# Second graph layer: the order of TensorE's edge products and of ScalarE's message scaling within a turn

## The reference, cut to what matters

```
h  = relu(layernorm(x))
h  = relu([h, mean of h[src] over dst, mean of h[dst] over src] @ W1 + b1)
y  = x + [h, mean of h[src] over dst, mean of h[dst] over src] @ W2 + b2
h2 = relu(layernorm(y))
agg = segment_sum(edge_attr, dst)
out = y + mlp([h2, agg, u])          # 256, 256, 128; leaky relu
```

## Time and profile before

| what | us |
|---|---|
| median of 3 runs | 4304.13 |
| lowest and highest run | 4294.77, 4335.73 |
| the profiled execution, its own time | 4353.21 |
| span of that execution | 4351.6 |
| granted TensorE clock, mean share of full speed | 0.93 |

### The profile page before, as it was taken

How to read it: one execution, slowest core, us unless ns; L and a number is a source line. 1 busy time by engine, 2 the same in 40 slices (tenths; PEclk the granted TensorE clock), 3 DMA queues, 4 the chain that set the end, 5 groups by cost and what they waited for, 6 DMA issues and landing times.

```text
span 4351.6 us, 100093 instructions
## 1 busy us (share of the span) xinstructions
PE 3767.9 (87%) x25698; PEld 3324.9 (76%) x25698; DVE 3179.5 (73%) x11005; ACT 2323.0 (53%) x5788; POOL 3002.4 (69%) x2962
## 2 busy tenths in 40 slices
PE   3385899899999688888888888879999999999999
PEld 0123788888888678887788788768888888888888
DVE  3284788888888555555555555569999999999998
ACT  0001444444444455555555555557777777777776
POOL 6614787787777677777777777756666666666665
PEclk6687999999999899999999999989999999999999
DMA  7714777777777577777777777767777777777765
GB/s 278 272 58 161 176 171 175 180 173 179 171 175 177 132 179 179 186 184 187 177 181 183 178 182 186 173 144 159 158 160 157 159 159 158 160 158 158 159 158 124
DMA packets 818323, 742.05 MB, mean 171 GB/s; under 512 B 200444, under 2 KB 629896, under 8 KB 818282
## 3 DMA queue, kind: packets, MB, share of 16 engines
q1 hardware_dynamic: 637702, 522.72, 40.8%
q0 software_dynamic: 166208, 167.10, 26.3%
q10 hardware_dynamic: 14372, 51.75, 3.0%
HBM read 355.07 MB, written 334.83 MB: 159 GB/s over the span
## 4 chain that ended last, share of the span: by engine, by line
PE 47%; issue 5%; another core or an unknown queue 4%; ACT 3%; DVE 3%; DMA 2%; SPq 1%; POOL 0%; ACTq 0%; DVEq 0%; POOLq 0%
PE bank L1559 8%; PE bank L1573 4%; PE bank L1572 4%; PE bank L1574 4%; PE bank L1444 3%; PE bank L1467 3%; PE bank L1468 3%; PE bank L1478 2%; PE bank L1537 2%; PE bank L1530 2%; PE bank L1536 2%; PE bank L1532 2%; PE bank L1531 2%; PE bank L1546 2%
## 5 line engine op out<-in xcount | busy, mean ns | idle before, releaser
L626 POOL DMA_INDIRECT node<-summed,rep_index x392 | 628.0, 1602 | 266.3 <-issue 129.4
L579 POOL DMA_INDIRECT sums<-summed,rep_index x392 | 620.7, 1583 | 166.9 <-issue 127.7
L657 POOL TENSOR_TENSOR resid<-node_out,b3s 128x128 f32<-128x128 f32 x784 | 336.7, 460 | 478.3 <-DVE rows L1281 474.9
L1231 DVE SCALAR_TENSOR_TENSOR z<-bank,bias,small 128x512 f32<-128x512 f32 x784 | 567.9, 744 | 67.6 <-ACT small L889 58.7
L889 ACT ACTIVATE small<-bank,bias_small 128x512 f32<-128x512 f32 x784 | 535.2, 683 | 106.8 <-PE bank L1574 59.3
L1467 PE MATMUL bank<-hx,W1s 128*128 128x128 f32 x1568 | 345.1, 306 | 221.5 <-ACT hx L830 179.8
L667 POOL TENSOR_TENSOR z_lo<-z,z_hi 128x512 fp32r<-128x512 f32 x392 | 496.4, 1287 | 9.5 <-ACT z_hi L920 9.5
L611 POOL DMA_INDIRECT ends<-sums,index x392 | 382.0, 974 | 121.9 <-issue 120.1
L1467 PEld LDWEIGHTS bank<-hx,W1s 128*128 128x128 f32 x1568 | 268.6, 215 | 254.5 <-issue 254.1
L1559 PE MATMUL bank<-w3s,z 128*128 128x128 f32 x3136 | 382.4, 275 | 3.1 <-DVE z L1231 3.1
L1559 PEld LDWEIGHTS bank<-w3s,z 128*128 128x128 f32 x3136 | 365.7, 192 | 4.1 <-DVE z L1231 4.0
(11 more groups left out here) (152 smaller groups left out, 9727.2 us busy)
## 6 DMA issues: line engine op xcount, KB each, us to landing
node<-blank SPq DMA_DIRECT2D x98, 768.0 KB
sums<-zeros ACTq DMA_DIRECT2D x98, 512.0 KB
normed<-in_x_dram SPq DMA_DIRECT2D x196, 256.0 KB
rows<-sums SPq DMA_DIRECT2D x196, 256.0 KB
y<-node_out SPq DMA_DIRECT2D x196, 256.0 KB
node_out<-node SPq DMA_DIRECT2D x196, 256.0 KB, 3.2
node_out<-y POOLq DMA_DIRECT2D x196, 256.0 KB, 4.2
a_parts<-a_pair SPq DMA_DIRECT2D x784, 64.0 KB, 2.5
```

The lines of the kernel that those rows point to most:

```text
L579: pool.indirect_dma_start(sums1, bass.IndirectOffsetOnAxis(ap=rep_index[:, b, s:s + 1], axis=0), summed[:, b, s, 0:F], None, compute_op=AL ...
L626: pool.indirect_dma_start(node1, bass.IndirectOffsetOnAxis(ap=rep_index[:, b, s:s + 1], axis=0), summed[:, b, s, :], None, compute_op=ALU. ...
L1231: dve.scalar_tensor_tensor(out=z[:, m, :], in0=bank[first_bank + m][:], scalar=bias[:, m:m + 1], in1=small[:, m, :], op0=ALU.add, op1=ALU. ...
```

## The change

Two moves, one in each of two streams; no instruction is added or removed.

- TensorE: `end_products`(g+1) goes from just behind `sums`(g) to just behind `x_transposes`(g+1, 1). The preactivations of block 0 and the transposes of block 1 so come ahead of it.
- ScalarE: `end_messages`(g+1) goes from just behind `normalised`(g+1, 1) to just behind `hidden_x`(g+1, 1), the last place but one of the turn.

```diff
@@ scalar stream, layer2, step @@
                         hidden_x(g + 1, 1 - b, 0)
                         end_rows(g + 1, 1 - b)
                         normalised(g + 1, 1 - b, 1)
-                        end_messages(g + 1, 1 - b)
                     if second:
                         root(g + 2, b, 0)
                     if follows:
                         hidden(g + 1, 1 - b, 0)
                         hidden_x(g + 1, 1 - b, 1)
+                        end_messages(g + 1, 1 - b)
                     if second:
                         normalised(g + 2, b, 0)
@@ tensor stream, layer2, step @@
                     sums(g, b, uses)
                     if follows:
-                        end_products(*ahead)
                         preactivations(*ahead, uses + b, 0)
                         x_transposes(*ahead, 1)
+                        end_products(*ahead)
                     node_products(g, b, 1)
```

## The result

The changed kernel takes 4295.12 us (median of 10 runs, 4276.09 to 4303.86), the kernel before 4319.72 (10 runs, 4294.77 to 4335.73). The ratio is 0.9935, with a 95% interval of 0.9915 to 0.9955: 0.65% faster, 28 us by the ratio and 25 by the medians. The forecast was 4299 us, 5 us under a median of three runs that lay low; seven more runs moved the median of before up by 16 us. The time was met, and the difference was five times the one forecast.

The account below looks back on a forecast made before the run. The prediction took a 12.30 us ring around block 0's x load, plus late events, to hold the 14.10 us turn. Its terms summed to -11 us, half expected lost: -5 us on 4304.13, hence 4299, 8-in-10 range 4245 to 4350.

Parts of the forecast that it names:

- ScalarE, the gain: ScalarE, messages taken from ahead of block 0's root: about 0.9 us gained in one turn of eight, 11 us in all.
- The forecast's own sign: In the changed kernel's trace: block 0's root directly behind `normalised`, with a wait longer by about 1.1 us.
- the guess of one turn in eight: Share of turns where block 0's root has its input ready when the messages end; bounds none and one in three.
- TensorE, priced at nothing: TensorE, block 0's preactivations and block 1's transposes start 0.91 us earlier but meet ScalarE at the root: no gain.
- rival A: Faster: `hidden`'s 47 unexplained waits shrink by 0.91 us each, 43 us (4261), at most 112.4 us (4192); chance 0.22.
- The covers: Slack before TensorE's transposes takes up ScalarE's later work: 1.32 us, 0.29 left; if gone, up to 101 us slower.
- Rival B: Slower: ScalarE's messages wait in their new place for late edge products, past 0.29 us of cover: 51 us (4355); chance 0.15.
- The ring around the x load: Chain from `node_rows` through block 0's x load, statistics and root back to `node_rows`: 12.30 us of the 14.10 us turn.
- Rival C: Faster: the messages' 1.12 us leave the path to `hx` in each turn, 110 us (4194); chance 0.02.

Follow-up runs that it names:

- The filler: The changed kernel with four activations that nobody reads put at the messages' old place, ahead of the root of block 0: 4282.29 us, ratio 0.9909.

## Why the prediction was right, and where it was not

The time lay in the range, and the size of the effect under the 1% that the forecast called no change. That 4299 came within 4 us of 4295.12 is luck: the base was 16 us too low and the gain 20 us too small, and the two errors nearly cancelled. The turn of 13.72 us stayed just inside the 13.7 at which the forecast would have failed. Point by point:

- **ScalarE, the gain.** "The root could start 1.1 us earlier if its input were there. It is not." The filler confirms it: 1.2 us of work put back there is free. The forecast's own sign held too: the root of block 0 waited 102 us in the stage before and 262 after, 1.7 us a turn more. Even the guess of one turn in eight was met, by 12 of 96. What the term left out is the wait ahead of the messages. The step priced `end_messages` by its 1.12 us and not by what it waits for: with a late completion the messages and the root come one after the other behind it, where now the root is done before. That wait was in the trace of before (37.9 us in the stage), and I had passed over it. ScalarE's half measured 11 to 20 us, where the sum had 11 and halved it.
- **TensorE, priced at nothing.** "The earlier `c_pre` and `c_xT` meet a ScalarE that stands at the root: nothing." This is the step that failed. With ScalarE's half in place, the earlier completions took `hidden`'s unexplained waits from 78 us to 39.4 and 26.3, and the time down by about 0.4%, 17 us. It is the mechanism of rival A, of which the prediction had worked out 43 us for its near end; TensorE's half gave two fifths of that, and only with ScalarE's half beside it. Alone it cost 43 to 48 us, which no part of the prediction foresaw. The waits also did not shrink each by 0.91 us, as A had it: there were 18 where there had been 47, at the same 2.2 to 2.4 us each, and part of them came up at the messages. The row of the changed kernel that answers to the earlier trace rows:

```profile
L838 ACT ACTIVATE hT<-bank,b1col x196: 667/687/707, 1465.4 to 2791.4; 128x512 f32<-128x512 f32 x196
...
  remote: 39.4, 18
```

- **The covers.** The 0.29 us left before the transposes held only in part. TensorE's transposes waited for `resid` 24.0 us in 32 cases, where it had been 2.2 us:

```profile
L1455 PE MATMUL bank<-ident,resid x784: 272/273/475, 1434.4 to 2787.3; 128*128 128x128 f32 x196
...
  ACT resid L820: 24.0, 32
```

- **Rival B** happened, but small: the messages wait 42.9 us for late completions in 25 cases, with the covers behind them. Its 51 us did not come, since about as much leaves `hidden`.
- **What bounds the kernel.** The ring around the x load, 12.30 us, was read correctly row by row and is not the bound: a smaller and an earlier load both failed to help. Rows that follow each other closely had made a chain, but the chain's waits only move. What does move the turn is a gather less on POOL: 1.0 to 1.2 of its 1.29 us come back. POOL's own stream is still not the bound: with three gathers its rows give 12.83 - 1.29 = 11.54 us, and the turn stays at 12.8.
- **Rival C** was excluded for the right reason: the root had a wait of its own in 84 of 96 turns before.

Left open is why completions are late. They go with POOL's gathers, but one gather less takes away both time on POOL and traffic, and no run separates the two.

## What to carry to other kernels

Price a moved step in an in-order stream by the wait in front of it as well as by its own time. Work is free in the shadow of a later wait. Work behind a wait that may end late is not, because what stands behind it is then done after the wait instead of before. And when two streams are reordered as a pair, the halves can have opposite signs; here TensorE's half alone was 1.0% slower, and the pair 0.65% faster. A ring that adds up in the timeline is a bound only after one has made a link of it shorter.

## What the runs showed of the hardware

TensorE's completions can reach the other engines much later than its recorded matmuls end: 4.3 us in the window shown (2416.5 to 2420.84). In the stage such waits of `hidden` came to 112.4 us before, 39.4 after, and with three gathers a turn 37.9 in the old order and 4.3 in the new. The trace gives them no owner. Leaving out one of POOL's gathers, 1.29 us of its stream and the traffic with it, took 1.2 us off the turn in the kernel before, although the engine, gaps included, was occupied for only 91% of 1500 to 2500 us there.
